# Two max tiles of a step in neighbouring PSUM banks, reduced by one VectorE instruction

## What is computed

```python
ada = silu(c) @ Wada + bada                       # shift, scale, gate, twice
h = layernorm(x) * (1 + scale_msa) + shift_msa
q, k, v = h @ Wq + bq, h @ Wk + bk, h @ Wv + bv   # 16 heads of 32
A = softmax(q @ k.T / sqrt(32))                   # per head, 2048 x 2048
x = x + gate_msa * (A @ v @ Wo + bo)
h2 = layernorm(x) * (1 + scale_mlp) + shift_mlp
out = x + gate_mlp * (gelu(h2 @ W1 + b1) @ W2 + b2)
```

## Time and profile before

| | us |
|---|---|
| median of 3 runs | 2406.3 |
| lowest and highest | 2401.29, 2407.16 |
| profiled execution, device time | 2402.13 |
| its span | 2400.3 |

### The profile page before, as it was taken

How to read it: one execution, slowest core, us unless ns; L and a number is a source line. 1 busy time by engine, 2 the same in 40 slices (tenths; PEclk the granted TensorE clock), 3 DMA queues, 4 the chain that set the end, 5 groups by cost and what they waited for, 6 DMA issues and landing times.

```text
span 2400.3 us, 48498 instructions
## 1 busy us (share of the span) xinstructions
PE 2350.2 (98%) x19312; PEld 1337.6 (56%) x19312; DVE 1749.9 (73%) x2866; ACT 1403.4 (58%) x2593; POOL 1675.0 (70%) x806
## 2 busy tenths in 40 slices
PE   6999989999999999999999999999999989999998
PEld 4788864444444444444444444444444458888887
DVE  4445748888888888888888888888888756556653
ACT  3232317777777777777777777777777742222221
POOL 0001029999999999999999999999999932233320
PEclk9999999999999999999999999999999999999999
DMA  8566463323323232322323232322323232222210
GB/s 279 184 208 200 134 170 74 82 66 70 82 64 85 61 86 61 79 61 60 78 59 81 56 78 61 79 61 61 78 58 77 69 84 81 71 71 71 71 36 35
DMA packets 211341, 211.16 MB, mean 88 GB/s; under 512 B 118557, under 2 KB 151325, under 8 KB 201961
## 3 DMA queue, kind: packets, MB, share of 16 engines
q1 hardware_dynamic: 204898, 200.91, 32.1%
q0 software_dynamic: 3936, 5.53, 1.0%
q10 hardware_dynamic: 2280, 1.63, 0.3%
HBM read 147.11 MB, written 60.59 MB: 87 GB/s over the span
## 4 chain that ended last, share of the span: by engine, by line
PE 92%; DMA 2%; DVE 2%; ACT 2%; issue 1%; SPq 0%; ACTq 0%; POOL 0%
PE ps L1435 21%; PE ps L1292 19%; PE ps L1411 11%; PE ps L1399 11%; PE ps L1542 7%; PE ps L1424 7%; PE ps L1413 6%; PE ps L1415 5%; PE ps L1420 3%; PE ps L1301 1%; DMA q_lo<-work 1%; ACT work L891 1%; DMA k_lo<-work 1%; PE ps L1332 1%; DVE work L1223 0%
## 5 line engine op out<-in xcount | busy, mean ns | idle before, releaser
L1130 DVE TENSOR_REDUCE part_max<-ps 128x1 f32<-128x512 f32 x1968 | 1222.3, 683 | 261.4 <-PE ps L1399 261.4
L913 ACT ACTIVATE work<-ps 128x512 f32<-128x512 f32 x2048 | 1057.7, 604 | 332.1 <-PE ps L1420 291.1
L754 POOL TENSOR_TENSOR work<-work 128x1024 f32<-128x1024 f32 x314 | 741.3, 2417 | 26.3 <-ACT work L913 25.9
L754 POOL TENSOR_TENSOR gate<-gate,work 128x1024 f32<-128x1024 f32 x288 | 674.7, 2393 | 12.8 <-ACT work L913 12.8
L1435 PE MATMUL ps<-work 128*32 128x512 f32 x4096 | 545.6, 605 | 0.2 <-ACT work L913 0.2
L1399 PE MATMUL ps<-acts_r 32*128 32x512 f32 x1328 | 413.4, 471 | 2.0 <-ACT work L913 0.5
L1292 PE MATMUL ps<-acts_r,weights_r 128*128 128x512 f32 x1536 | 378.3, 397 | 9.3 <-DVE acts_r L1040 3.8
L1292 PEld LDWEIGHTS ps<-acts_r,weights_r 128*128 128x128 f32 x1536 | 289.8, 190 | 72.4 <-ACT work L891 4.7
L1411 PEld LDWEIGHTS ps<-acts_r 32*128 32x128 f32 x1408 | 142.8, 182 | 305.2 <-DVE part_max L1130 174.3
L1411 PE MATMUL ps<-acts_r 32*128 32x512 f32 x1408 | 292.2, 465 | 2.6 <-ACT work L913 1.7
L1413 PE MATMUL ps<-acts_r 32*128 32x512 f32 x1408 | 253.0, 393 | 0.0
(11 more groups left out here) (104 smaller groups left out, 2827.5 us busy)
## 6 DMA issues: line engine op xcount, KB each, us to landing
acts_r<-k_lo SPq DMA_DIRECT2D x124, 256.0 KB, 4.6
acts_r<-k_hi SPq DMA_DIRECT2D x120, 256.0 KB, 4.6
work<-in_x SPq DMA_DIRECT2D x16, 1024.0 KB, 5.8
q_hi<-work SPq DMA_DIRECT2D x32, 256.0 KB, 2.8
q_lo<-work SPq DMA_DIRECT2D x32, 256.0 KB, 3.4
k_hi<-work SPq DMA_DIRECT2D x32, 256.0 KB, 2.6
k_lo<-work SPq DMA_DIRECT2D x32, 256.0 KB, 3.3
v_rows<-work SPq DMA_DIRECT2D x32, 256.0 KB, 2.0
```

The costliest lines, as they stand in the source:

```text
L754: nc.gpsimd.tensor_tensor(acc[:, at], first, prob[:, t % RING, at], ALU.add).then_inc(add_ok, 1)
L913: nc.scalar.activation(prob[:, t % RING, j * CH:(j + 1) * CH], ps[:, bank, :], ACT.Exp, scale=SCALE).then_inc(exp_ok, 1)
L1130: nc.vector.tensor_reduce(part_max[:, r * TT + q // NQ, q % NQ:q % NQ + 1], ps[:, bank, :], AX.X, ALU.max).then_inc(a_max, 1)
```

## The change

In the planner max tile 0 is marked free at 13 rather than 11 (the mark of tile 1), and max tiles 0 and 1 no longer take the bank marked free first, each for itself. They take two neighbours, `first` and `first + 1`: the neighbours whose later mark is earliest. In `quad` VectorE reduces tiles 2 and 3 as before, waits until both tiles 0 and 1 are there, and reduces both with one instruction of 128 x 2 x 512, which writes two columns of `part_max` and raises `a_max` by two when it ends.

```diff
-    until = {"S": (8, 10, 12, 14), "M": (11, 13, 6, 8), "D": 16}
+    until = {"S": (8, 10, 12, 14), "M": (13, 13, 6, 8), "D": 16}
...
                 if (g or t) and g < G - 2 or g == G - 2 and t < NT - LEAD:
+
+                    first = min(range(BANKS - 1), key=lambda b: max(free[b], free[b + 1]))
                     for r in others:
-                        uses["max"][r] = use("M", now + until["M"][r], banks)
+                        uses["max"][r] = use("M", now + until["M"][r], banks if r > 1 else range(first + r, first + r + 1))
...
             def quad(uses, g, q):
 
-                for r, (bank, _, n) in zip((2, 3, 0, 1), uses):
+                row, key = q // NQ, slice(q % NQ, q % NQ + 1)
+                for r, (bank, _, n) in zip((2, 3), uses):
                     dve.wait_ge(a_mm, n)
-                    nc.vector.tensor_reduce(part_max[:, r * TT + q // NQ, q % NQ:q % NQ + 1], ps[:, bank, :], AX.X, ALU.max).then_inc(a_max, 1)
+                    nc.vector.tensor_reduce(part_max[:, r * TT + row, key], ps[:, bank, :], AX.X, ALU.max).then_inc(a_max, 1)
+                (bank, _, _), (_, _, n) = uses[2:]
+                dve.wait_ge(a_mm, n)
+                nc.vector.tensor_reduce(part_max[:, row:row + TT + 1:TT, key], ps[:, bank:bank + 2, :], AX.X, ALU.max).then_inc(a_max, 2)
```

## The result

| | before | after |
|---|---|---|
| median, us | 2404.25 (4 runs) | 2680.07 (4 runs) |
| lowest to highest | 2401.29 to 2407.16 | 2673.16 to 2683.57 |
| profiled execution | 2402.13 | 2678.87 |
| its span | 2400.3 | 2677.0 |

The ratio is 1.1146, with an interval of 1.113 to 1.1162: the kernel became 11.5% slower, by 276 us. The forecast was 2663, in a range of 2605 to 2715.

A forecast was written before the change was run, and what follows sets the result against it. TensorE was taken to bound the kernel, busy for 98% of the span. Bank waits of 75 + 92 + 90 + 4 = 261 us, added to the profiled 2402.1, gave 2663 us, in a range of 2605 to 2715.

The forecast's parts named there:

- late steps: 384 of 492 attention steps whose max tile pair would wait longer for a bank, on max tile 3 or a score.
- Which wait sets a step: On TensorE, the second max tile's wait for its bank lengthens the step in full, as values need all row groups.
- The banks: Pair's latest predecessor by the planner's loop: max tile 2 in 108 steps, max tile 3 in 123, score 0 in 258, score 1 in 3.
- The prices: Extra wait per step: max tile 3 0.61 us; score 0 0.67, or 0.74 behind a sum; score 1 1.22.
- max 3: Steps where the pair waits for VectorE's reduction of max tile 3: 123 x 0.61 = 75 us.
- The joint instruction costs nothing: VectorE's joint reduction, taken as 1.22 us, would neither lengthen nor shorten the path.
- 22 us for the pair that is held 0.41 us into the next step: First pass of scores 2 and 3 0.07 us late in at most 309 steps; counted only for the range's high end.
- the 34 us of VectorE's time: 492 fewer VectorE instructions at perhaps 0.07 us each; off the path, a gain only if VectorE were the bound (3%).
- score 0 behind a sum: After a step with a sum, the pair waits for score 0's exponential on ScalarE: 121 x 0.74 = 90 us.
- The clock: Rival: TensorE's clock falls to its lower level in one step in four, 270 us more, 2930 us; 5%.
- the three signs of being wrong: Max tiles 0 and 1 start by 1.3 in most steps; values no longer follow scores by 0.4; clock leaves 1.00.
- 8 rather than 6: Planner's marks for when banks come free: 8 for a pair with max tile 3 or score 0, 6 with max tile 2.

The follow-up runs named there:

- Turning the order round: Last pass of scores 2 and 3 queued ahead of max tiles 0 and 1: in the changed kernel 2674.03 us, in the kernel before 2402.65 us.
- the joint instruction on banks free in time: Changed kernel with a planner that hands out all seven banks of a step at once, spare bank beside max tile 2's: 2418.46 us.
- the mark alone: Kernel before with only the planner's mark of max tile 0 raised from 11 to 13, no pairs, four single reductions: 2411.61 us.

## Why the prediction was right, and by how much it missed

The mechanism was the one forecast, and the count of late steps with their prices held: 261 us predicted, 277 measured in the profiled executions. One term was taken from a step that does not stand for its whole set, and the trace of the kernel before had shown that.

- **Which wait sets a step.** Right. Turning the order round left the time within 6 us in the changed kernel and where it was in the kernel before, so it is the second max tile and not the score pass beside it.
- **The banks.** Right. The banks without the joint instruction cost 264 us; the joint instruction on banks free in time is 14 us above before, and no different from single ones (2418.46 and 2419.05).
- **The prices.** Right within 0.03 us each by their medians. Placed in all steps, max 3 gives 0.58 a step where 0.61 was the term.
- **The joint instruction costs nothing.** Nearly right: about 11 us between the two medians. The prediction had kept 22 us for the pair that is held 0.41 us into the next step; 5 us of it are seen step by step, so the cover is not quite whole. What it did have wrong is the 34 us of VectorE's time. In a run of four each reduction starts 0.60 after the one before, and the four take 2.49; two and the joint one take 1.29 and 1.23, so 2.52. The busy time fell by 0.8 us. The sum did not use this term.
- **The forecast is 16 us low.** The term that was mis-sized is score 0 behind a sum: 90 predicted, 100 measured. Of its 121 steps 15 are the second step of a head (head 2 and the odd ones from 3), and they cost 1.23 each in the median and 1.49 in the mean, where the other 106 cost 0.73. ScalarE copies out values and a sum one after the other in every head's second step, and starts its first exponential 1.86 us into it, not 1.37. Max tile 1 starts at 2.51. That makes 7 us (15 x 0.49); another 4 us are falls of the clock in six of these steps. With the rest of the clock's price (9.5 us in all, see below) the two account for the 16 us; what is left cancels.

The timelines of ScalarE and TensorE in such a step (head 7) of the changed kernel:

```profile
763.80 0.60 ACT L881 ACTIVATE work<-ps 128x512 f32<-128x512 f32 x1 [0.32 <-PE ps L1430]
764.30 0.59 ACT L893 ACTIVATE work<-ps 128x512 f32<-128x512 f32 x1
764.92 0.48 ACTq L895 DMA_DIRECT2D partial_sums<-work  x1
765.53 2.31 ACT L915 ACTIVATE work<-ps 128x512 f32<-128x512 f32 x4 [0.64 <-ACT work L893]
```

```profile
763.67 0.50 PE L1405 MATMUL ps<-acts_r,w_r 32*128 32x512 f32 x2
...
766.18 0.50 PE L1405 MATMUL ps<-acts_r,w_r 32*128 32x512 f32 x1 [0.75 <-ACT work L915]
```

The same step in the kernel before, ScalarE and TensorE:

```profile
702.33 0.60 ACT L879 ACTIVATE work<-ps 128x512 f32<-128x512 f32 x1 [0.34 <-PE ps L1424]
702.82 0.59 ACT L891 ACTIVATE work<-ps 128x512 f32<-128x512 f32 x1
703.44 0.48 ACTq L893 DMA_DIRECT2D partial_sums<-work  x1
704.05 2.07 ACT L913 ACTIVATE work<-ps 128x512 f32<-128x512 f32 x4 [0.64 <-PE ps L1420]
```

```profile
702.19 0.50 PE L1411 MATMUL ps<-acts_r 32*128 32x512 f32 x2
...
704.91 0.50 PE L1411 MATMUL ps<-acts_r 32*128 32x512 f32 x2
```

ScalarE starts its first exponential 1.86 us into the step here too (704.05 less 702.19), and the step lasts 2.72 all the same: max tile 1 waits for no exponential in it, so the delay costs nothing there. The prediction read ScalarE's start in one step behind a sum and took it for all 121. A look at each place within a head would have given 15 of them their 1.23.

- **The clock.** Given 5%, with 270 us. It did not happen at that size, but it happened in small: in the attention stage of the changed kernel's profiled execution the granted clock fell to its lower level nine times, eight times for 3.4 us and once for 6.8, and not once in that of the kernel before. Seven of the falls cost 9.5 us (below).
- **The signs.** Of the three signs of being wrong one came true, "if the clock leaves 1.00", and it was too strict: the clock's part is some 10 us. All 384 late steps have a max tile that starts at 1.89 us or later. In 290 of them it is both tiles; in the other 94 tile 0 starts early, as in the second kind shown above, at the same price.

## What to carry to other kernels

When two tiles must lie side by side for one instruction, price the banks first: on the same free banks the merged instruction saved nothing (2418.5 against 2419.1 us), while a worse predecessor in one bank cost 0.6 to 0.7 us in 384 of 492 steps. A planner that compares times at which banks come free must also know when the queue comes to the tile; "8 rather than 6" looks small, but both lay behind the need at 4.5, so the difference was paid in full. And a delay on an engine with cover (ScalarE's copies at a head's start) becomes a cost as soon as a new wait is hung on that engine: read its worst step, not only a typical one.

## What was not expected of the hardware

TensorE's clock fell in the changed kernel in the second step of heads 5, 9, 13, 17, 21 and 23, that is in the steps with the longest wait, and in a few others. Busy time by stretch of the changed kernel, the second to fourth steps: head 7 without a fall, and head 5 with one; the granted clock is the third number from the end:

```profile
763.67:773.91 10.24, 9.43 (x96) 3.88 (x93) 7.54 (x9) 7.39 (x14) 5.84 (x3) 1.00 0.27 60
646.77:658.45 11.68, 10.87 (x98) 4.52 (x95) 7.54 (x9) 7.39 (x14) 5.68 (x3) 0.85 0.35 81
```

The same three steps take 11.68 us instead of 10.24. TensorE's timeline shows what it did before the fall, and values at the lower level:

```profile
648.04 0.49 PE L1405 MATMUL ps<-acts_r 32*128 32x512 f32 x1
649.28 0.50 PE L1405 MATMUL ps<-acts_r 32*128 32x512 f32 x1 [0.74 <-ACT work L915]
649.71 1.87 PE L1441 MATMUL ps<-work 128*32 128x512 f32 x8
```

TensorE had no matmul for 0.74 us; then values took 1.87 us, where the others take 1.06. Counted in this way, against the same steps of heads without a fall, the six falls in second steps cost 1.2 to 1.4 us each, and one in head 29's third step 1.2: 9.5 us together. The other two, in the second step of head 0 and in the last head, are not in this sum. They need no late pair: the kernel before with the turned order has a fall in head 0's second step too (that head took 2.5 us longer than before), and the run with the mark alone has one in the last head. With max tile 1 on the bank of max 3 in every step, all of them late by 0.6, the clock fell at these two places only; with score 0, eleven times, nine of them in the second or third step of a head. So in these runs the falls stand at the longest waits, and not where waits are only many. The Trainium skill (TensorE: Matmul & The Clock Gate, A second HAM failure mode: psum-queue depth-cycling) tells that short idles from cycling through PSUM banks let the clock swing; the trace agrees that it falls, nine times, and shows that the price here is some 10 of 277 us. Why it falls in some of the like steps and not in the others was not tested.
